# Widening the edge-count matrix in its own order, and reading it with a step in the products

## The reference

```python
def reference(x, src, dst, edge_weight, L0_gnn_bias, W_self0, W_neigh0, b0, W_self1, W_neigh1, b1):
    h = jnp.maximum(_layernorm(x, axis=-1), 0.0)                # x: 1250 x 1024
    W = jnp.zeros((1024, 1024)).at[src, dst].add(edge_weight)   # 40,000 edges
    x = x + (h @ W.T + L0_gnn_bias)
    h = jnp.maximum(_layernorm(x, axis=-1), 0.0)
    # two layers over the graph (src, dst), deg = edges into each node, at least 1:
    #   layer(h) = h @ W_self + (segment_sum(h[src], dst) / deg) @ W_neigh + b
    h1 = relu(layer(h, W_self0, W_neigh0, b0))
    return x + layer(h1, W_self1, W_neigh1, b1)
```

## Time and profile before

| what | value |
|---|---|
| times of three runs | 802.75, 804.55, 811.87 us |
| median | 804.55 us |
| the profiled execution: span from the first to the last instruction | 802.3 us (its own time is not listed apart from the span) |
| TensorE busy with products | 769.9 us (96%) |
| ScalarE busy | 370.8 us (46%) |
| line 1160, widening, 40 times | 106.6 us |
| line 1493, products with A, 820 records | 18% of the chain of work that ended last |

### The profile page before, as it was taken

How to read it: one execution, slowest core, us unless ns; L and a number is a source line. 1 busy time by engine, 2 the same in 40 slices (tenths; PEclk the granted TensorE clock), 3 DMA queues, 4 the chain that set the end, 5 groups by cost and what they waited for, 6 DMA issues and landing times.

```text
span 802.3 us, 13275 instructions
## 1 busy us (share of the span) xinstructions
PE 769.9 (96%) x4553; PEld 639.1 (80%) x4554; DVE 485.3 (60%) x720; ACT 370.8 (46%) x526; POOL 412.3 (51%) x569
## 2 busy tenths in 40 slices
PE   3878999999999999999999999999999999999998
PEld 2767888888888888888887888888888888887787
DVE  7989377777554788867413342136568766246444
ACT  7757634333364232223246886453233223347653
POOL 5000167676649899765742210127899756724311
PEclk9689999999999999999999999999999999999999
DMA  3112456775565853577855654566745659667654
GB/s 111 42 57 92 137 178 192 237 228 186 191 225 193 275 169 116 182 230 269 278 180 189 210 158 105 171 209 229 261 134 164 202 198 332 216 206 268 223 163 142
DMA packets 83239, 151.40 MB, mean 189 GB/s; under 512 B 10979, under 2 KB 21278, under 8 KB 83168
## 3 DMA queue, kind: packets, MB, share of 16 engines
q1 hardware_dynamic: 61646, 102.65, 40.8%
q10 hardware_dynamic: 20002, 42.91, 15.0%
q0 software_dynamic: 1520, 4.92, 1.5%
HBM read 103.79 MB, written 46.65 MB: 188 GB/s over the span
## 4 chain that ended last, share of the span: by engine, by line
PE 82%; DVE 8%; DMA 3%; POOL 3%; issue 2%; ACT 2%; POOLq 0%; SPq 0%; ACTq 0%; DVEq 0%
PE bank L1449 45%; PE bank L1493 18%; PE bank L1384 13%; DVE L L1676 2%; DVE R L1661 2%; PE bank L1280 1%; PE bank L1296 1%; DVE L L1668 1%; PE bank L1510 1%; DMA cst<-prod1g_scratch 1%; DMA b<-in_L_gnn_b 1%; PE bank L1377 1%; PE bank L1275 1%; POOL split L935 1%; ACT Ax L1160 1%
## 5 line engine op out<-in xcount | busy, mean ns | idle before, releaser
L1449 PE MATMUL bank<-slot,split 128*128 128x512 f32 x1680 | 386.3, 390 | 0.2 <-POOL split L935 0.2
L1449 PEld LDWEIGHTS bank<-slot,split 128*128 128x128 f32 x1680 | 313.7, 188 | 66.0 <-issue 1.5
L897 POOL TENSOR_TENSOR AT<-AT,az 128x50 int32 (+3 forms) x288 | 95.5, 332 | 119.7 <-DMA az<-asum_scratch 78.7
L935 POOL TENSOR_TENSOR split<-stage,split 128x512 fp32r<-128x512 f32 x50 | 66.5, 1331 | 116.9 <-ACT split L1128 116.8
L1160 ACT CAST Ax<-AT 128x1280 fp32r<-128x1280 uint16 x40 | 106.6, 2667 | 34.5 <-PE bank L1493 27.5
L1811 DVE TENSOR_TENSOR slot<-T,slot 128x512 fp32r<-128x512 f32 x64 | 90.1, 1430 | 23.8 <-ACT slot L1119 22.0
L1384 PE MATMUL bank<-slot,split_m 128*128 128x512 f32 x320 | 91.2, 396 | 0.0
L1933 DVE SCALAR_TENSOR_TENSOR cst<-bank,dinv,stage 128x512 f32<-128x512 f32 (+1 forms) x41 | 30.3, 738 | 94.8 <-PE bank L1493 94.6
L1128 ACT CAST split<-stage 128x512 fp32r<-128x512 f32 x50 | 31.1, 624 | 118.1 <-PE bank L1449 67.4
L1493 PE MATMUL bank<-slot,Ax 128*128 128x512 f32 (+1 forms) x336 | 77.6, 383 | 0.4 <-ACT Ax L1160 0.4
L952 POOL TENSOR_TENSOR T<-T,wst 128x512 f32<-128x512 f32 x48 | 69.4, 1462 | 5.2 <-DMA wst<-in_L_gnn_W_self 5.2
(11 more groups left out here) (193 smaller groups left out, 1030.6 us busy)
## 6 DMA issues: line engine op xcount, KB each, us to landing
stage<-hT_scratch SPq DMA_DIRECT2D x90, 256.0 KB, 3.6
wst<-in_L_gnn_W_neigh SPq DMA_DIRECT2D x56, 256.0 KB, 4.3
wst<-in_L_gnn_W_self SPq DMA_DIRECT2D x56, 256.0 KB, 3.3
x1b_scratch<-x ACTq DMA_DIRECT2D x10, 512.0 KB, 6.1
hT_scratch<-hTs ACTq DMA_DIRECT2D x10, 512.0 KB, 3.2
stage<-prod0s_scratch SPq DMA_DIRECT2D x20, 256.0 KB, 3.0
hT_scratch<-h1s ACTq DMA_DIRECT2D x20, 256.0 KB, 3.5
stage<-prod1s_scratch SPq DMA_DIRECT2D x20, 256.0 KB, 2.7
```

Source lines behind the costliest of these rows:

```text
L897: pool.tensor_tensor(a, a, az32[:, n % NZ, pairs * pos:pairs * (pos + 1)], ALU.add) \
L935: pool.tensor_tensor(split[:, v % 2, 1, :], source(v), split[:, v % 2, 0, :].bitcast(F32), ALU.subtract).then_inc(s_olo, 1)
L1449: last = pe.matmul(dense_bank(v, which)[:, :], split[:, v % 2, a, NT * k:NT * (k + 1)], slot[t % 2][:, b, HF * (HK * which + k):HF * (HK * ...
```

## The change

`Ax` and `Axlo` keep their sizes and places, but the order of their two inner dimensions is turned: from source tile x destination to destination x source tile, which is the order of `AT`. The widening then reads 1,280 adjacent numbers and writes 1,280 adjacent ones, where it read with a step of ten numbers (20 bytes) before. The stationary operand of a product, the 128 destinations of one source tile, was 128 adjacent numbers and is now 128 numbers with a step of ten (40 bytes). The moving operand, the number of instructions, their order on each engine and all waits stay as they are.

```diff
-        Axlo = sb("Axlo", [NT, TN, NT], F32R)
+        Axlo = sb("Axlo", [NT, NT, TN], F32R)
...
-        Ax = sb("Ax", [NT, 2, TN, NT], F32R)
+        Ax = sb("Ax", [NT, 2, NT, TN], F32R)
...
-                act.copy(Ax[:, o % 2, :, :], ATd[:, NT * n:NT * (n + 1), :].rearrange("p d s -> p s d")).then_inc(s_ax, 1)
+                act.copy(Ax[:, o % 2, :, :], ATd[:, NT * n:NT * (n + 1), :]).then_inc(s_ax, 1)
...
-                            last = pe.matmul(halves_bank(rest_o, part)[:, cols], Ax[:, o % 2, s, :],
+                            last = pe.matmul(halves_bank(rest_o, part)[:, cols], Ax[:, o % 2, :, s],
...
-                                last = pe.matmul(halves_bank(rest_o, part)[:, cols], Axlo[:, s, :],
+                                last = pe.matmul(halves_bank(rest_o, part)[:, cols], Axlo[:, :, s],
...
-                    dve.tensor_tensor(Axlo[:, :, :], ATd[:, NT * n:NT * (n + 1), :].rearrange("p d s -> p s d"),
+                    dve.tensor_tensor(Axlo[:, :, :], ATd[:, NT * n:NT * (n + 1), :],
                                       Ax[:, o % 2, :, :].bitcast(F32), ALU.subtract).then_inc(s_axlo, 1)
```

## The result

The changed kernel takes 821.43 us in the median of 4 runs (819.9 to 822.54) against 804.7 us (802.75 to 811.87): a ratio of 1.02, 95% interval 1.0154 to 1.0246, 16.7 us more. It is slower clear of the noise; whether by a little under or over 2% the interval leaves open. The profiled execution of after took 819.9 us, with a span of 817.9 us; that of before has a span of 802.3 us.

The account below looks back on a forecast made before the run. TensorE's products, busy 96% of the span, were taken as the bound. Last tile +3.9, 18 tile starts +2.0, 762 products nothing, widening -1.5: +4.4 us on 804.55 gave 809 us, range 802 to 832 us.

Parts of the forecast that it names:

- the last tile: 40 products of 256 columns at the chain's end: 218 ns loads exceed their 120 ns cover, +3.9 us.
- the first rival: Every product of line 1493: stepped load outruns its cover from 2.08 times; at 2.25 times +19.6 us, 824 us; chance 0.34.
- The widening: ScalarE's line 1160: 1,284 ns in place of 2,667, mostly beside other work; two TensorE waits go, gain 1.5 us.
- The uncovered loads of 18 tiles: First-layer tiles that begin behind transposes: each first load takes 218 ns in place of 109, uncovered, +2.0 us.
- The 762 products of 512 columns: Line 1493 outside the other two load terms: the 218 ns load stays under 227 ns of product, costing nothing.
- the threshold of 2.08: Line 1493, 512 columns: a 109 ns load may become 2.08 times as long, 227 ns, before anything moves.
- 13 ns fixed: Line 1493's products: 0.42 ns a column, plus a fixed 13 ns each.
- The sign that the prediction gave: Line 1493's weight loads, shown as 188 ns before, were to be shown longer by about 109 ns.
- slack on the way to TensorE: Reason for loads at 2.0, under ScalarE's 2.25 times: the moving operand arrives at 0.42 ns a number, loads take 0.85.
- The estimate of 838 us: Upper end of the slower case for line 1493's loads, from a VectorE page's 2.4 times for stepped reads.
- The other rivals: ScalarE's widening doesn't get shorter, 806 to 810.5 us; or the stepped widening disturbs TensorE, 0.7 us faster, chance 0.03.

Follow-up runs that it names:

- run 2: Changed kernel with its new widening, but products reading 128 adjacent (wrong) numbers of the buffer; 803.9 us, ratio 0.9979.
- run 7: Changed kernel with its last tile in one part, 20 products of 512 columns in place of 40 of 256, and one store; 817.69 us, ratio 1.0149.
- run 6: Changed kernel with load steps 1 to 10 by tile, all products 512 columns, moving operand one number read 512 times; one execution, 806.5 us.
- experiment 4: Changed kernel with load steps 1 to 10 by tile and the second layer's products cut to 128 columns; one execution, 813.55 us.

## Why the prediction was right in its range and wrong in its mechanism

The measured 821.43 us lie within the stated range, 802 to 832 us, and the kernel became slower as forecast. But the forecast value was 809 us, with a mechanism that did not hold: the loads were to stay under the products, and +4.4 us to come from the last tile and the starts of 18 tiles, less the gain of the widening. Measured are +16.7 us, 11.6 of them in the term that was put at nothing. The range holds the time because it took in the first rival, at a chance of 0.34.

*The widening* was right: 1,264 ns where 1,284 were worked out, all of it off the path but for two waits, and 1.55 us of gain where 1.5 were forecast (run 2).

*The uncovered loads of 18 tiles* were right: from the first to the second product it is 440 ns where it was 315, so 18 x 125 = 2.3 us where 2.0 were forecast. The first product behind the transposes is shown for 0.60 us, where it was 0.48:

```profile
429.66 0.60 PE L1493 MATMUL bank<-g_mid,Ax 128*128 128x512 f32 x1
```

*The last tile* was right: 20 x (229 - 120) + 20 x (236 - 120) = 4.5 us where 3.9 were forecast, and run 7 gets 3.5 of it back.

*The 762 products of 512 columns* are the step that failed: "the load, 218 ns, stays under 227 ns. Nothing." Measured, it is 17.6 ns each in the second layer (244.3 against 226.7, some 380 products, 6.7 us) and some 13 in the first (the phase's 7.2 us less the 2.3, over some 380 products, 4.9 us). Two things in that step were wrong. The load's own time is 227 to 229 ns, 2.1 times the adjacent one, and not 2.0: the threshold of 2.08 was already reached. That alone would cost at most 2 ns a product, 229 against 227. The rest, some 16, is the other thing: a load under a product of 512 columns isn't free even where it is shorter. It costs 6 ns at a step of two, where it is 119 ns long, and at step ten the two together need 244, which is 15 to 17 more than either. The rows of before held a hint of that, misread: of the "13 ns fixed" in 227 = 214 + 13, 11 go when the moving operand stays in one place (run 6).

The sum by its own terms, with what was measured: 11.6 + 4.5 + 2.3 - 1.5 = 16.9 us; the phases have 16.85, the medians 16.7. Of these terms the first layer's 4.9 us are what its phase leaves over, so only the second layer's part of the agreement is a test: 6.7 + 4.5 - 1.5 = 9.7 us, and its phase has 9.65.

The sign that the prediction gave, the load's shown duration, misleads as a measure of the load alone. It grew by 136 ns (324 against 188), which on 109 ns would be 2.25 times; the narrow products and run 6 show 2.1.

One reading of rows was off without effect: a span of 802.3 us does not put the profiled execution beside the fastest run of 802.75, since the span is about 2 us shorter than the time (817.9 against 819.9 in after).

*The first rival* named the place, and its price (824 us) was near. Its mechanism was half right: ScalarE's ratio of 2.25 would have given 245 ns for the load alone, and the distance is 244, but the load alone has 2.1 times and the rest is the meeting of two reads. That its price fits is partly luck. The load alone did come out below that ratio, but no run shows that slack on the way to TensorE is the reason. The estimate of 838 us in the prediction supposed 2.4 times, which is too high. The Trainium skill's page "SBUF — State Buffer", section "Specifications (TRN2)", has lines of 16 bytes, with two accesses to a line needed for full bandwidth. The table agrees for the load alone: 4-byte numbers with steps of 1 and 2 take 112 and 119 ns, of 3, which leaves some lines with one, 176, and from 4 on, one number a line, 221 to 241.

The other rivals: the widening did get shorter; no disturbance by the old widening was found (in run 2 a tile of the first layer takes 5.02 us, as before, and the phase is not shorter, 101.31 us against 100.53).

Open is why steps of 4, 8 and 9 cost more than 5, 6 and 10, why the delay between the two reads nearly vanishes at step 4, and which places in memory make TensorE's two reads meet; no run varied the places. No version here is measurably faster than the kernel before: run 2 shows that a faster widening, got in any way, is worth about 1 to 1.5 us. That this could be had by moving the two late widenings ahead of the rounding in ScalarE's queue was not tried.

## What to carry to other kernels

Before a rearrangement is moved from an engine with time to spare into an operand of TensorE, count how often each side reads: here 40 widenings got 1.4 us shorter off the path, and 820 loads on the path got twice as long. Here a weight load with 4-byte numbers four to ten apart took 221 to 241 ns, about as long as a product of 512 columns, so it needed more cover than such a product gave. And leave a margin: here a load of 119 ns under a product of 512 columns still cost 6 ns, so "shorter than its cover" is not "free".

## What was not expected of the hardware

TensorE's weight load and moving operand delay each other at 512 columns: with a load of 119 ns (step 2) products of float32r are 233 ns apart, and 216 when the moving operand is one number read again and again. Even with both read without a step it is 227 against 216. An adjacent load goes by the engine's clock (109 to 112 ns at 2.4 GHz, 213 at 1.2 GHz), while one with a step of 4 or more takes its 225 to 241 ns at both levels. And the clock fell to 1.2 GHz at 720.8 in experiment 4, in the third tile of 128-column products (steps 1 to 3, from 713.24 on), where 256-column products with a step of ten, 229 to 236 ns apart, kept 2.4 GHz through the last tile of the changed kernel.
